# A two-layer decoder block: the order of all engines in the first attention, its PSUM banks, and its crossing into the FFN stage

## The chip, the cores and the metric

The kernel runs on one core of a Trainium2 chip. Time is device microseconds of one execution, lower is better. The engines are TensorE (PE), VectorE (DVE), ScalarE (ACT), GpSimd (POOL) and SyncE (SP, which here only issues DMAs). Each takes its own instructions in the written order, and they meet only at semaphores.

## The reference, cut to what matters

Sixteen sequences of 128 rows by 128 columns pass through four steps, each added to its input. The first one is the stage that the change touches:

```python
# x: (16, 128, 128), ctx: (16, 120, 128), H = 16 heads of 8
xn = layernorm(x)
q, k, v = xn @ Wq.T, ctx @ Wk.T, ctx @ Wv.T          # split into 16 heads
scores = einsum('bhqd,bhkd->bhqk', q, k) * SCALE      # + causal mask
attn = softmax(scores)
x = x + einsum('bhqk,bhkd->bhqd', attn, v) @ Wo.T
x = x + ternary_ffn(layernorm(x))                     # 128 -> 512 -> 128
x = x + relative_attention(layernorm(x), ctx)         # 16 heads of 64
x = x + int8_linear(layernorm(x))
```

The FFN needs its two weight matrices turned into ternary ones first (mean of the absolute values, comparison, sum with the rest). The last step needs its matrix quantised. Both are done once, in small pieces strewn among the steps of the first attention.

## The kernel before

Every engine runs three stages one after the other: `attn0` (first attention), `ffn0`, and `layer1` (second attention and last linear). Each stage is a software pipeline over the 16 sequences: at step s it works on several sequences t at once (for example scores of t = s, softmax sums and the scaling of t = s-1, the product with V of t = s-2, the output projection of t = s-3, layer norm of t = s+3 and s+4). Steps 6 to 11 of `attn0` are a hardware loop, the others are written out. The order inside a step is fixed by hand, engine by engine. `crossing` is the list of how the last steps of `attn0` and the first of `ffn0` alternate on each engine.

One step of `attn0` holds, for each sequence: on PE two pairs of masks (`causal`), two pairs of score products (32 rows of the array each, output tile 0 to 3 = head groups g of 4 heads), two groups of 16 transposes of the probabilities (64 rows), two groups of 8 products with V (`vexp`, 32 columns), three projections q, k, v, the projection `wo`, and a transpose of `xn` (all 128x128). On ACT 16 exponentials and two half copies of the transposes. On DVE four maxima (`nmax`), four reciprocals (`rsum`), two half copies (`probT` and its second half, which lies in `relr0`), copies `oT`, `qT`, `kexp` (which lies in `relw`), `v`, `xnT`, the layer-norm statistics and `xn`. On POOL four multiplications of the probabilities by `rsum` (`scaled0` to `scaled3`), `vexp`, and a power for the layer norm (`rstd`).

The pieces of work done once stand on DVE at steps 2 to 5 (comparison of `wup` and `wdn`, into `hsq` and `relw0`) and 12 to 14 (`qx`), on POOL at steps 12, 13, 14 and 17.

`after(e, sem, n)`, `freed` and `wait_ge` are waits. In `ffn0`, DVE's first instruction of step s waits for `root`, POOL's power for the layer norm of sequence s+2, and that power is in POOL's step s-1 of `ffn0`.

Of the kernel before, what the change touches and what calls it, by code (L numbers as in the profile page):

```python
# [19 lines left out]
def decoder_kernel(nc, x, ctxT, mask, wq0T, wk0T, wv0T, wo0T, wupT, wdnT, wq1, wk1, wv1, wr1, ub, vb,  # L20
# [7 lines left out]
    with ctx:  # L28
# [270 lines left out]
        def _(pool):  # L299
# [133 lines left out]
        def _(act):  # L433
# [11 lines left out]
            def attn0(s, par):  # L445
# [6 lines left out]

                t, p = s - 2, par
                if on(t):
                    act.wait_ge(A0["probT_ps"], 2 * t + 1)
# [1012 lines left out]
```

## Time and profile before

| | us |
|---|---|
| three runs | 459.0, 452.06, 458.26 |
| their median | 458.26 |
| the profiled execution | 454.79 |
| its span, first to last instruction | 453.0 |
| of it attention steps, about | 8 to 120 |
| of it the crossing into the FFN stage, about | 112 to 135 |
| mean granted TensorE clock | 0.981 |

The profile is of one execution. Its time is 1.79 us over its span, and lies between the runs' lowest and their median. Starts and durations below are of that execution.

### The profile page before, as it was taken

Reading aid. Unit: us, or ns where it says so; the run is one execution under the profiler, and the core shown is the slowest. Engines: PE = TensorE matmul, PEld = TensorE weight load, DVE = VectorE, ACT = ScalarE, POOL = GpSimd, SP = SyncE. Lnnn points to the kernel's source line nnn. Section 1 sums busy time; section 2 is a strip of 40 time slices with the busy share of each in tenths; the row PEclk is TensorE's granted clock in tenths of the full one; section 3 lists DMA queues with packets and bytes.
Section 4 is the critical chain, followed back from the end, with each engine's and each line's share of the span. In section 5 each row is a group of like instructions: output and inputs, shape, how many; then the busy total and the mean of one; then the engine's idle time right before and its main releaser. Section 6 shows DMA issues by size and latency. Waiting matters only on the chain.

```text
span 453.0 us, 16761 instructions
## 1 busy us (share of the span) xinstructions
PE 415.2 (92%) x6147; PEld 313.1 (69%) x6147; DVE 398.8 (88%) x1300; ACT 375.1 (83%) x1483; POOL 264.2 (58%) x370
## 2 busy tenths in 40 slices
PE   7999999998789998889999999989999989998871
PEld 6555556555457777778888877868887878887560
DVE  5899999989679985799789999999999999999855
ACT  1999999998845556699989989988998999898941
POOL 4388888878966640044346357447447545646775
PEclk9999999999899999999999999999999999999796
DMA  7250000000000005887447564754754754764000
GB/s 213 58 193 26 14 11 6 11 8 15 2 2 0 0 2 138 216 208 205 120 106 191 156 146 120 190 133 104 198 134 110 198 147 94 186 163 100 8 7 23
DMA packets 54392, 44.88 MB, mean 99 GB/s; under 512 B 43952, under 2 KB 49328, under 8 KB 54320
## 3 DMA queue, kind: packets, MB, share of 16 engines
q1 hardware_dynamic: 53616, 43.59, 37.8%
q8 instruction: 46, 0.75, 0.7%
q10 hardware_dynamic: 704, 0.32, 0.3%
q14 instruction: 26, 0.21, 0.2%
HBM read 22.92 MB, written 20.97 MB: 97 GB/s over the span
## 4 chain that ended last, share of the span: by engine, by line
PE 44%; DVE 44%; issue 4%; ACT 3%; POOL 2%; DMA 1%; SPq 1%; POOLq 0%; DVEq 0%; ACTq 0%
PE PS L1003 37%; DVE prob L855 3%; PE PS L1019 3%; DVE xf L906 2%; DVE prob L901 2%; PE PS L1213 2%; DVE prob L989 1%; DVE nmax L861 1%; PE PS L1179 1%; DVE prob L995 1%; DVE prob L878 1%; DVE prob L865 1%; DVE prob L867 1%; DMA wr<-in_wr 1%; DVE qu L896 1%
## 5 line engine op out<-in xcount | busy, mean ns | idle before, releaser
L381 POOL TENSOR_TENSOR prob<-prob,rsum 128x480 f32<-128x480 f32 x64 | 69.1, 1091 | 85.4 <-DVE rsum L846 80.9
L533 ACT ACTIVATE prob<-prob,nmax 128x120 f32<-128x120 f32 x256 | 102.3, 440 | 1.0 <-DVE nmax L937 1.0
L449 ACT ACTIVATE prob<-PS,nmax 128x120 f32<-128x120 f32 x256 | 89.6, 394 | 4.3 <-DVE nmax L769 2.6
L324 POOL TENSOR_TENSOR prob<-prob,rsum 128x480 f32<-128x480 f32 x64 | 62.5, 988 | 23.2 <-DVE rsum L742 12.8
L533 ACT ACTIVATION_READ_ACCUMULATOR prob<-prob,nmax 128x1 f32 x256 | 63.0, 246 | 0.0
L449 ACT ACTIVATION_READ_ACCUMULATOR prob<-PS,nmax 128x1 f32 x256 | 61.5, 240 | 0.0
L1003 PE MATMUL PS<-rT,qv 64*32 64x152 f32 x2048 | 42.7, 293 | 5.8 <-DVE uo L933 3.8
L1003 PEld LDWEIGHTS PS<-rT,qv 64*32 64x32 f32 x2048 | 30.6, 105 | 21.6 <-issue 18.5
L1003 PEld LDWEIGHTS PS<-xnT,wq 128*128 128x128 f32 x288 | 37.1, 191 | 8.8 <-issue 7.3
L1003 PE MATMUL PS<-xnT,wq 128*128 128x128 f32 x288 | 42.7, 284 | 0.1
L1003 PE MATMUL PS<-ctx,wk 128*128 128x120 f32 x288 | 41.0, 278 | 0.0
L1003 PE MATMUL PS<-wv,ctx 128*120 128x512 f32 (+1 forms) x96 | 40.3, 501 | 0.0
L1003 PE MATMUL PS<-probT,hv 120*64 120x128 f32 x512 | 36.4, 286 | 3.2 <-ACT probT L618 3.2
L1003 PE MATMUL PS<-kT,qu 64*128 64x120 f32 x512 | 35.8, 279 | 3.0 <-ACT relw L632 2.0
L1003 PEld LDWEIGHTS PS<-ctx,wk 128*128 128x128 f32 x288 | 35.9, 191 | 2.2 <-issue 2.2
L1003 PE MATMUL PS<-wo,oT_pairs 128*128 128x128 f32 x256 | 35.9, 284 | 1.0 <-ACT oT_pairs L568 1.0
L1003 PE MATMUL PS<-relw,qT 32*128 32x480 f32 x128 | 34.4, 613 | 0.4 <-DVE relw L747 0.4
L1003 PEld LDWEIGHTS PS<-probT,hv 120*64 120x64 f32 x512 | 28.3, 140 | 8.8 <-ACT probT L618 3.7
L1003 PEld LDWEIGHTS PS<-kT,qu 64*128 64x128 f32 x512 | 31.5, 188 | 4.2 <-ACT relw L632 2.6
L1003 PEld LDWEIGHTS PS<-wo,oT_pairs 128*128 128x128 f32 x256 | 31.9, 196 | 2.5 <-ACT oT_pairs L568 1.8
L1019 PEld LDWEIGHTS PS<-ident,prob 64*120 64x120 f32 x512 | 18.2, 138 | 19.1 <-issue 19.1
L416 POOL TENSOR_TENSOR rstd<-ve,mhalf 128x1 f32<-128x1 f32 x16 | 8.7, 544 | 34.4 <-DVE ve L660 34.4
(195 smaller groups left out, 1128.5 us busy)
## 6 DMA issues: line engine op xcount, KB each, us to landing
rel_scratch<-relw SPq DMA_DIRECT2D x128, 152.0 KB, 3.1
relr<-rel_scratch SPq DMA_DIRECT2D x64, 240.0 KB, 4.2
ctx<-in_ctxT SPq DMA_DIRECT2D x32, 60.0 KB, 1.9
out_x<-fin SPq DMA_DIRECT2D x16, 64.0 KB, 3.2
x_all<-in_x SPq DMA_DIRECT2D x1, 640.0 KB, 7.1
wr<-in_wr SPq DMA_DIRECT2D x1, 512.0 KB, 5.4
wq<-in_wq SPq DMA_DIRECT2D x1, 512.0 KB, 3.6
wk<-in_wk SPq DMA_DIRECT2D x1, 512.0 KB, 4.4
```

What stands on the lines that cost most here:

```text
L324: return pool.tensor_tensor(pr, pr, cols(rsum[p], g, HG).unsqueeze(2).to_broadcast([S, HG, SK]), ALU.mult)
L381: return pool.tensor_tensor(pr, pr, cols(rsum[p], g, HG).unsqueeze(2).to_broadcast([S, HG, SK]), ALU.mult)
L416: pool.tensor_tensor(rstd[p][:, 0:1], ve[p][:, 0:1], mhalf[:, :], ALU.pow).then_inc(A1["rstd"], 1)
L449: last = act.activation(cols(prob[p], n, SK), cols(scores, q, SK), ACT.Exp, bias=nmax[p][:, n:n + 1], accum_out=ssum[p][:, n:n + 1])
L533: last = act.activation(cols(pr, n, SK), cols(pr, n, SK), ACT.Exp, bias=bias[:, n:n + 1], accum_out=total[:, n:n + 1])
L855: dve.scalar_tensor_tensor(out=sc, in0=cap[p][:, :].unsqueeze(1).to_broadcast([S, HG, SK]), scalar=NEG, in1=sc, op0=ALU.add, op1=ALU.min). ...
L861: dve.tensor_reduce(out=cols(nmax[p], 1, HG), in_=heads(cols(prob[p], 1, HG * SK), HG), op=ALU.max, axis=AX.X, negate=True).then_inc(A1["n ...
L901: dve.scalar_tensor_tensor(out=sc, in0=cap[p][:, :].unsqueeze(1).to_broadcast([S, HG, SK]), scalar=NEG, in1=sc, op0=ALU.add, op1=ALU.min). ...
L906: dve.tensor_scalar(xf[p][:, :], row(x_all, t), mv3[p][:, 0:1], rstd3[p][:, :], ALU.subtract, ALU.mult)\
L1003: return pe.matmul(o, a, b, start=start, stop=stop)
L1019: last = pe.transpose(PS[0:SK, bank, q * S // 2:(q + 1) * S // 2], cols(prob[p], g * HG + q, SK)[rows], ident_sb[rows, rows])
L1213: last = pe.transpose(PS[0:SK, bank, q * S // 2:(q + 1) * S // 2], cols(prob[p], g * HG + q, SK)[rows], ident_sb[rows, rows])
```

## The change

The four compute engines get a new order within a step of `attn0`. PE's list changes the tile shape (128x128, 32 rows, 64 rows, 32 columns) 8 times in a step, where it did 9 times. PSUM banks are given out anew. POOL does `vexp` and the scaling of group 3 after the fourth reciprocal, directly before and after that of group 2. DVE does `oT` after both late maxima, and `xn` directly behind the fourth reciprocal. In `crossing`, POOL's first two `ffn0` steps move behind one more `attn0` step each, and DVE's first one moves behind `attn0(14)`. Nothing is added to or taken from the computation.

```diff
@@ -323,14 +323,8 @@
-                t, p = s - 2, par
-                if on(t):
-                    scale_probs(p, 3).then_inc(A0["scaled3"], 1)
-                t, p = s - 1, 1 - par
-                if on(t):
-                    after(pool, A0["av1"], t - 1)
-                    pool.tensor_tensor(vexp[p][:, :].rearrange("p (g c) -> p g c", g=G), v_sb[p][:, :].unsqueeze(1).to_broadcast([SK, G, D]),
-                                       vmask_sb[:, :].rearrange("p (g c) -> p g c", g=G), ALU.mult).then_inc(A0["vexp"], 1)
...
@@ -342,7 +336,10 @@
                 t, p = s - 1, 1 - par
                 if on(t):
                     pool.wait_ge(A0["rsum"], 4 * t + 4)
+                    scale_probs(p, 3).then_inc(A0["scaled3"], 1)
                     scale_probs(p, 2).then_inc(A0["scaled2"], 1)
+                    pool.tensor_tensor(vexp[p][:, :].rearrange("p (g c) -> p g c", g=G), v_sb[p][:, :].unsqueeze(1).to_broadcast([SK, G, D]),
+                                       vmask_sb[:, :].rearrange("p (g c) -> p g c", g=G), ALU.mult).then_inc(A0["vexp"], 1)
@@ -361,10 +358,10 @@
 
             def crossing():
                 attn0(14, 0)
+                attn0(15, 1)
                 ffn0(-3, 1)
-                attn0(15, 1)
+                attn0(16, 0)
                 ffn0(-2, 0)
-                attn0(16, 0)
                 attn0(17, 1)
                 ffn0(-1, 1)
                 attn0(18, 0)
...
@@ -824,8 +827,8 @@
 
             def crossing():
+                attn0(14, 0)
                 ffn0(-3, 1)
-                attn0(14, 0)
                 attn0(15, 1)
                 ffn0(-2, 0)
                 attn0(16, 0)
```

PE's own crossing is as it was; only what its FFN steps wait for follows the new banks. Three places show what the orders come to.

PE, one step of the first attention (step 3, word for word in its written order; `relr,vexp` and `probT,vexp` are the products with V, `ident,prob` the transposes). Before:

```order
L1003 MATMUL PS<-causal,ident_bf 128x480 [waits a0_probs] x2
L1003 MATMUL PS<-wo,oT 128x128 [waits attn0_output_weights,a0_oT,a0_scaled2]
L1003 MATMUL PS<-relw,qT 128x480 [waits a0_kexp]
L1019 MATMUL PS<-ident,prob 120x64 [waits a0_scaled3,a0_probT1,ident_bf_set]
L1003 MATMUL PS<-xnT,wq 128x128 [waits a0_probT0,a0_xnT,a0_ctx_loaded0]
L1003 MATMUL PS<-causal,ident_bf 128x480 [waits a0_probs] x2
L1003 MATMUL PS<-probT,vexp 32x128 [waits a0_x_done,a0_probT0]
L1003 MATMUL PS<-relw,qT 128x480 x2
L1129 MATMUL PS<-ident,xn 128x128 [waits a0_probT3,a0_xn]
L1003 MATMUL PS<-relr,vexp 32x128 [waits a0_probT3,a0_probT2]
L1019 MATMUL PS<-ident,prob 120x64 [waits a0_scaled0,a0_scaled1,a0_v,ident_bf_set]
```

After:

```order
L1006 MATMUL PS<-wo,oT 128x128 [waits attn0_output_weights,a0_oT]
L1006 MATMUL PS<-relw,qT 128x480 [waits a0_kexp,a0_scaled3]
L1022 MATMUL PS<-ident,prob 120x64 [waits a0_probT1,a0_scaled2,a0_probT0,ident_bf_set]
L1006 MATMUL PS<-probT,vexp 32x128 [waits a0_x_done,a0_vexp]
L1006 MATMUL PS<-xnT,wq 128x128 [waits a0_v,a0_xnT,a0_ctx_loaded0]
L1006 MATMUL PS<-causal,ident_bf 128x480 [waits a0_probs]
L1117 MATMUL PS<-ident,xn 128x128 [waits a0_probT3,a0_xn]
L1006 MATMUL PS<-relw,qT 128x480 x2
L1006 MATMUL PS<-relr,vexp 32x128 [waits a0_probT3,a0_probT2]
L1022 MATMUL PS<-ident,prob 120x64 [waits a0_scaled0,a0_scaled1,a0_xnT,ident_bf_set]
```

The transpose of `xn` now follows the second pair of masks, which has its own shape, and the first products with V stand ahead of the projections.

DVE at step 3 of the first attention, where one of the four pieces of FFN weight work stands (`hsq<-wup`). Before:

```order
L704 TENSOR_REDUCE nmax1<-PS 128x4 [waits a0_scores0]
L706 TENSOR_REDUCE nmax1<-PS 128x4
L721 SCALAR_TENSOR_TENSOR hsq<-wup,tiny0,hsq 128x512
L737 TENSOR_SCALAR qT0<-PS 128x128 [waits a0_qkv_ps,setup_vector]
L740 RECIPROCAL rsum0<-ssum0 128x4
L742 RECIPROCAL rsum0<-ssum0 128x4 [waits a0_probs]
```

After:

```order
L729 RECIPROCAL rsum0<-ssum0 128x4 [waits a0_probs]
L733 TENSOR_SCALAR xn0<-x_all,mv0,rstd0 128x128 [waits a0_rstd]
L748 SCALAR_TENSOR_TENSOR hsq<-wup,tiny0,hsq 128x512
L764 TENSOR_SCALAR qT0<-PS 128x128 [waits a0_qkv_ps,setup_vector]
L768 COPY xnT1<-PS 128x128 [waits a0_xnT_ps]
L773 TENSOR_TENSOR relw0<-PS,kmask 128x480
L778 TENSOR_REDUCE nmax1<-PS 128x4 [waits a0_scores1]
L780 TENSOR_REDUCE nmax1<-PS 128x4
L676 RECIPROCAL rsum1<-ssum1 128x4 [waits a0_probs]
L680 COPY oT1<-PS 128x128 [waits a0_av1]
```

The piece moved from behind two maxima to behind the fourth reciprocal (L729) and `xn`, and `oT` now comes last of the chain maxima, reciprocal, `oT`.

POOL in the crossing, around `rstd<-ve,half`, which is the `root` that DVE's FFN steps wait for. Before:

```order
L357 TENSOR_TENSOR rstd0<-ve0,half 128x2 [waits f0_var,setup_pool]
L324 TENSOR_TENSOR prob1<-prob1,rsum1 128x480
L332 TENSOR_TENSOR vexp0<-v0,vmask 120x512 [waits a0_av1]
L324 TENSOR_TENSOR prob0<-prob0,rsum0 128x480 [waits a0_rsum] x3
L357 TENSOR_TENSOR rstd1<-ve1,half 128x2 [waits f0_var]
```

After:

```order
L324 TENSOR_TENSOR prob0<-prob0,rsum0 128x480 [waits a0_rsum] x2
L324 TENSOR_TENSOR prob0<-prob0,rsum0 128x480
L341 TENSOR_TENSOR vexp0<-v0,vmask 120x512
L354 TENSOR_TENSOR rstd0<-ve0,half 128x2 [waits f0_var]
L324 TENSOR_TENSOR prob1<-prob1,rsum1 128x480 [waits a0_rsum] x3
L324 TENSOR_TENSOR prob1<-prob1,rsum1 128x480
L341 TENSOR_TENSOR vexp1<-v1,vmask 120x512
L354 TENSOR_TENSOR rstd1<-ve1,half 128x2 [waits f0_var]
L348 TENSOR_TENSOR wdn<-wdn,relw0 128x512
```

Each of the first two roots moved behind a whole attention step of POOL, the four scalings and `vexp`, and the second stands directly ahead of the last piece on `wdn`.

## Rows read from the trace of the kernel before

**Rows 1.** The chain of waits, 50 to 85 us: shares of that stretch.

```profile
by line: PE PS L1003 78.5%; PE PS L1019 18.2%; PE PS L1129 3.7%
```

**Rows 2.** Busy time of 50 to 75 us: PE, PEld, DVE, ACT, POOL, clock, DMA.

```profile
50.00:75.00 25.00, 25.00 (x307) 14.58 (x305) 23.77 (x80) 24.95 (x131) 21.24 (x23) 1.00 0.05 12
```

**Rows 3.** Timeline of PE: start, length, operation, tile, count; most of one step.

```profile
63.17 0.58 PE L1003 MATMUL PS<-causal,ident_bf 128*128 128x480 bf16 x2
63.58 0.38 PE L1003 MATMUL PS<-wo,oT 128*128 128x128 f32 x2
...
65.52 0.49 PE L1003 MATMUL PS<-xnT,wq 128*128 128x128 f32 x2
...
66.28 0.57 PE L1003 MATMUL PS<-causal,ident_bf 128*128 128x480 bf16 x2
66.78 0.64 PE L1003 MATMUL PS<-probT,vexp 120*32 120x128 f32 x16
67.36 1.07 PE L1003 MATMUL PS<-relw,qT 32*128 32x480 f32 x4
...
68.62 0.64 PE L1003 MATMUL PS<-relr,vexp 120*32 120x128 f32 x16
...
69.82 0.58 PE L1003 MATMUL PS<-causal,ident_bf 128*128 128x480 bf16 x2
```

**Rows 4.** Timeline of DVE in the same steps.

```profile
69.33 0.29 DVE L778 COPY oT<-PS 128x128 f32<-128x128 f32 x1
...
71.67 0.66 DVE L704 TENSOR_REDUCE nmax<-PS 128x4 f32<-128x480 f32 x1
72.24 0.65 DVE L706 TENSOR_REDUCE nmax<-PS 128x4 f32<-128x480 f32 x1
```

**Rows 5.** Timeline of PE at a wait for DVE; in brackets the idle time.

```profile
95.17 0.30 PE L1129 MATMUL PS<-ident,xn 128*128 128x128 f32 x1 [0.15 <-DVE relr L752]
```

**Rows 6.** Timelines of POOL and DVE: DVE operations that read SBUF, and POOL's beside them.

```profile
25.29 0.83 DVE L719 TENSOR_SCALAR hsq<-wup,tiny 128x512 f32<-128x512 f32 x1
...
32.29 0.74 DVE L721 SCALAR_TENSOR_TENSOR hsq<-wup,tiny,hsq 128x512 f32<-128x512 f32 x1
...
39.21 0.48 DVE L719 TENSOR_SCALAR relw<-wdn,tiny 128x512 f32<-128x512 f32 x1
...
20.27 0.99 POOL L324 TENSOR_TENSOR prob<-prob,rsum 128x480 f32<-128x480 f32 x1 [1.77 <-DVE rsum L742]
...
20.71 0.62 DVE L756 TENSOR_SCALAR xn<-x_all,mv,rstd 128x128 f32<-128x128 f32 x1
...
431.28 0.32 DVE L906 TENSOR_SCALAR xf<-x_all,mv_f,rstd_f 128x128 f32<-128x128 f32 x1
...
431.36 0.55 POOL L406 TENSOR_TENSOR x_all<-xb,uo 128x128 f32<-128x128 f32 x1
```

**Rows 7.** Timelines of POOL and DVE in the crossing.

```profile
113.24 0.71 POOL L357 TENSOR_TENSOR rstd<-ve,half 128x2 f32<-128x2 f32 x1
...
114.86 1.28 POOL L332 TENSOR_TENSOR vexp<-v,vmask 120x512 f32<-120x512 f32 x1
...
126.36 1.27 POOL L351 TENSOR_TENSOR wdn<-wdn,relw 128x512 f32<-128x512 f32 x1
...
116.38 0.17 DVE L765 RECIPROCAL rsum<-ssum 128x4 f32<-128x4 f32 x1
...
118.67 0.21 DVE L786 TENSOR_SCALAR tiny<-rstd 128x1 f32<-128x1 f32 x1
...
119.21 0.32 DVE L804 TENSOR_SCALAR xn<-x_all,mv,tiny 128x128 f32<-128x128 f32 x1
...
123.30 0.17 DVE L765 RECIPROCAL rsum<-ssum 128x4 f32<-128x4 f32 x1
...
125.42 1.07 DVE L804 TENSOR_SCALAR xn<-x_all,mv,tiny 128x128 f32<-128x128 f32 x1
126.41 1.24 DVE L808 TENSOR_SCALAR ve<-eps,mv 128x2 f32<-128x2 f32 x1
```

More of the change, by code:

```diff
@@ L700, in attn0 @@
                     dve.tensor_copy(ident_bf[:, :], ident_sb[:, :]).then_inc(ident_set, 1)
+                t, p = s - 2, par
+                if on(t):
+                    dve.wait_ge(A0["probT_ps"], 2 * t + 1)
+                    dve.tensor_copy(query_half(probT0[0], 1), heads(PS[0:SK, 6, :], 2 * HG)).then_inc(A0["probT1"], 1)
+                t, p = s - 1, 1 - par
+                if on(t):
+                    dve.wait_ge(A0["probs"], 4 * t + 2)
+                    dve.reciprocal(cols(rsum[p], 0, HG), cols(ssum[p], 0, HG)).then_inc(A0["rsum"], 1)
@@ L701, in attn0 @@
+                t, p = s - 3, 1 - par
+                if on(t):
+                    dve.wait_ge(A0["y_ps"], t + 1)
+                    if at_step(s, NB - 1):
+                        link(dve.tensor_copy(qrhs[:, :], PS[:, 7, D:2 * D]))
+                        link(dve.tensor_copy(rhs_scale[:, :], PS[:, 7, 2 * D:3 * D]))
+                    dve.tensor_tensor(row(x_all, t), PS[:, 7, 0:D], row(x_all, t), ALU.add).then_inc(A0["x_done"], 1)
                 t, p = s, par
                 if on(t):
+                    after(dve, A0["vexp"], t - 1)
+                    dve.tensor_copy(v_sb[p][:, :], PS[0:SK, 0, 256:256 + D]).then_inc(A0["v"], 1)
@@ new lines, in attn0 @@
+                t, p = s - 1, 1 - par
+                if on(t):
+                    dve.wait_ge(A0["probs"], 4 * t + 4)
+                    dve.reciprocal(cols(rsum[p], 3, HG), cols(ssum[p], 3, HG)).then_inc(A0["rsum"], 1)
+                t, p = s + 3, 1 - par
+                if on(t):
+                    dve.wait_ge(A0["rstd"], t + 1)
+                    dve.tensor_scalar(xn[p][:, :], row(x_all, t), mv[p][:, 0:1], rstd[p][:, 0:1],
+                                      ALU.subtract, ALU.mult).then_inc(A0["xn"], 1)
@@ L1050, in attn0 @@
                     pe.wait_ge(A0["kexp"], t + 1)
-                    for g, bank in ((0, 0), (1, 2)):
+                    for g, bank in ((0, 2), (1, 1)):
                         rows = slice(32 * g, 32 * g + 32)
@@ L1064, in attn0 @@
                 if on(t):
-                    free = held(pe, t + 1)
+                    count0 = held(pe, t + 1)
+                    count1 = held(pe, t + 1)
                     ready = held(pe, t + 1)
                     pe.wait_ge(ident_set, 1)
-                    pe.wait_ge(A0["probT1"], free)
-                    pe.wait_ge(A0["scaled3"], ready)
-                    probs_transpose(p, 2, (6, 5)).then_inc(A0["probT_ps"], 1)
+                    pe.wait_ge(A0["probT0"], count0)
+                    pe.wait_ge(A0["probT1"], count1)
+                    pe.wait_ge(A0["scaled2"], ready)
+                    probs_transpose(p, 2, (5, 6)).then_inc(A0["probT_ps"], 1)
+                if at_step(s, 2):
+                    pe.wait_ge(r_set, 4)
+                t, p = s - 2, par
+                if on(t):
+                    pe.wait_ge(A0["vexp"], t + 1)
+                    after(pe, A0["x_done"], t)
+                    for g in (0, 1):
+                        for q in range(HG):
+                            last = mm(PS[32 * q:32 * q + 32, 7, 0:S], vexp[p][:, g * D + 32 * q:g * D + 32 * q + 32],
+                                      cols(probT0[0], (g % 2) * HG + q, S), start=(g == 0), stop=(g == G - 1))
+                    last.then_inc(A0["av0"], 1)
                 if at_step(s, 1):
@@ L1096, in attn0 @@
                         pe.wait_ge(masks_loaded, 16 * 2)
-                    after(pe, A0["probs"], 4 * t)
                     mm(PS[:, 3, 0:HG * SK], ident_bf[:, :], causal_sb[:, :], stop=False)
-                if at_step(s, 2):
-                    pe.wait_ge(r_set, 4)
-                t, p = s - 2, par
+                t, p = s + 2, par
                 if on(t):
-                    pe.wait_ge(A0["probT0"], t + 1)
-                    after(pe, A0["x_done"], t)
-                    for g in (0, 1):
-                        for q in range(HG):
-                            last = mm(PS[32 * q:32 * q + 32, 7, 0:S], vexp[p][:, g * D + 32 * q:g * D + 32 * q + 32],
-                                      cols(probT0[0], (g % 2) * HG + q, S), start=(g == 0), stop=(g == G - 1))
-                    last.then_inc(A0["av0"], 1)
+                    pe.wait_ge(A0["xn"], t + 1)
+                    freed(pe, (A0["probT3"], t - 3, t - 4), (A0["xnT"], t, t - 1))
+                    pe.transpose(PS[:, 6, 0:S], xn[p][:, :], ident_sb[:, :]).then_inc(A0["xnT_ps"], 1)
                 t, p = s, par
                 if on(t):
-                    for g, bank in ((2, 3), (3, 1)):
+                    for g, bank in ((2, 3), (3, 4)):
                         rows = slice(32 * g, 32 * g + 32)
```

158 lines of the change are left out of this document (65 added, 93 removed), and 3 rows, old and new, of the table A0.

## The prediction, made before the changed kernel had run

> **What bounds it now.** I read the chain of waits over the steady attention steps first: every piece of it is PE work, none a wait for another engine [rows 1]. Then the busy times of the same stretch: PE 25.00 of 25 us, ACT 24.95, DVE 23.77, POOL 21.24, clock 1.00 [rows 2]. So PE sets the step, but nobody is far behind: DVE has 25 - 23.77 = 1.23 us idle in 3.76 steps, 0.33 us a step, and ACT shows none (its lengths stretch while it waits, so it may have some). PE's timeline gives the step: masks to masks 63.17 to 69.82, 6.65 us [rows 3]. A gain on PE can be no more than what the nearest other engine leaves.
>
> **PE's changes of shape.** The price of one is read from two pairs of the same masks. The pair at 63.17, followed by another 128x128 product, takes 0.41 us until the next start; that at 66.28, followed by products of another shape, takes 66.78 - 66.28 = 0.50 [rows 3]. So a change costs 0.09 us. One of nine goes (masks to the transpose of `xn`): PE's own work becomes 6.65 - 0.09 = 6.56 us a step. Over the 16 steps this is at most 1.5 us, 0.3%. The bounds of a change are 0.05 and 0.15, by the other joints in PE's timeline, hence 0.8 to 2.4 us. I take 1.5 as the gain on offer.
>
> **Who takes it back: the wait for `oT`.** In the new order a loop closes over PE and DVE: the late scores end, DVE takes two maxima, a reciprocal and `oT`, and only then may PE do `wo` and all that follows to the next late scores. Its length, by start to start: `wo`, early scores and 16 transposes 63.58 to 65.52, 1.94 us; first V products 66.78 to 67.36, 0.58; projections 65.52 to 66.28, 0.76; masks without a change 0.41; transpose of `xn` and late scores to their end, 67.36 to 68.62 and the 0.07 by which the scores' 1.07 exceeds 1.00, 1.33 [rows 3]. PE's part is 5.02. DVE's: two maxima of 72.24 - 71.67 = 0.57 each, a reciprocal that holds the next start for half of its 0.17, say 0.09, `oT` 0.29, and about 0.04 to start behind the scores: 1.56 [rows 4, 7]. Then PE restarts behind a wait for DVE with 0.15 idle [rows 5]. Sum 6.73 us, against 6.65 before and 6.56 on PE alone. The 0.15 is of a place where the shape changes too, which `wo` behind the masks does not; without the 0.09 of that it is 0.06, and the sum 6.64. So the step will be 6.6 to 6.75. I take 6.67: the loop is worth +0.02 a step, +0.3 us in 16 steps, bounds -1.2 and +2.4. The gain on PE is thus given back in a wait for `oT`, a resource that the old order had early.
>
> **The work done once, steps 2 to 5.** Here the queue matters. DVE's fourth reciprocal releases three POOL operations at a stroke in the new order (scaling 3, scaling 2, `vexp`), and behind it on DVE stand `xn` and then the weight piece. Rows show that such a DVE operation does not run beside a POOL one: `xn` started at 20.71, 0.44 us into a scaling that ran to 21.26, and took 0.62 where the like of it took 0.32 at 119.21; in the crossing one took 1.07 [rows 6, 7]. The blocked `xn` ended 0.07 us behind POOL's end (21.33 against 21.26); a 512-wide piece has more to do once it is let in, by estimate its own length less some 0.2 of start: 0.3 for a comparison (0.48), 0.55 for a three-operand piece (0.74). In the old place the four pieces took 0.83, 0.74, 0.48 and 0.74 us, the last alike the second [rows 6]. In the new place `xn` starts when half of the reciprocal's 0.17 us is over and POOL's first scaling when all of it is, 0.08 behind `xn`; it is itself held a little, say 0.1, and with its 0.99 ends about 1.17 behind `xn`'s start; so the two comparisons end at 1.47 from `xn`'s start and the two three-operand pieces at 1.72. Without that block they would end at 0.25 + their old length, 1.08, 0.73, 0.99 and 0.99. The difference is 0.39 + 0.74 + 0.73 + 0.73 = 2.6 us. DVE's slack of 0.33 a step was used up by the pieces themselves before, so the 2.6 pass on in full; if half a step's slack is still there it is 1.5. I take 2.6, bounds 0.5 and 3.5.
>
> The Trainium skill (SBUF — State Buffer, section "SBUF: two separate sides") says that VectorE and GpSimd share one port pair as an exclusive lock for a whole instruction, which goes to whoever starts first, when VectorE works in a two-port mode or with two SBUF inputs. The trace agrees at 20.71. By that rule the step's `xn` itself is at risk too, in all 13 steps; without the rule this edit would cost nothing, and the sum would be 2.6 us lower.
>
> **The crossing.** Before, POOL did the first root at 113.24, long before DVE asked at 118.67 [rows 7]. Now POOL's first root stands behind two scalings and `vexp` that wait for the fourth reciprocal of sequence 14. With that reciprocal where it was, 116.38: it ends at 116.55, then 0.95, 0.95 and 1.23 us (the 0.99 and 1.28 of the rows, less the overlap of one with the next) and the root of 0.71 give 120.4; DVE goes on at 120.45 instead of 118.67, +1.8 us. DVE stands still there with the last softmax work queued behind: the reciprocals, `oT` and the half copies of sequence 15 and 14, for which POOL and PE wait. Second round, first `xn` to second: DVE reaches the fourth reciprocal of sequence 15 after 3.0 us if nothing disturbs it (`ve`, reciprocal, `oT` and the first half copy 1.3, PE's 16 transposes and the restart 0.9, the second half copy and the reciprocal 0.8; before it took 123.30 - 119.21 = 4.09 with waits in it [rows 7]), then 0.17, again 3.84 on POOL, 0.54 from root to `xn` (119.21 - 118.67): 7.5 us, against 125.42 - 119.21 = 6.21. That is +1.3, up to +2.4. Third round: before, `xn` and `ve` at 125.42 and 126.41 took 1.07 and 1.24, held by a scaling and by the piece on `wdn` [rows 7]. Now the `wdn` piece starts at the root's end and holds `xn` alone, to about 1.35 behind the root; before it was 127.65 - 124.88 = 2.8 to the end of `ve`. It saves 1.2. Together +1.9. PE idles longer there and its granted clock may fall; I add nothing for that, but let the upper bound go to +5; the lower is 0. Steps 12 to 14 with the `qx` pieces are DVE-bound before and after, and I put them at 0, as I do the prologue (steps -4 to 1), where each new wait meets work that is one or two sequences short: +0.5, bounds -0.5 and +1.
>
> **The sum.** 0.3 + 2.6 + 1.9 + 0.5 = +5.3 us. FFN and second attention are unchanged and move along. Against the profiled execution: 454.79 + 5.3 = 460.1. That execution lies 3.5 us under the median of the runs shown (458.26) and the four times have a mean of 456.0; with the change on these two it is 461.3 to 463.6. I forecast **462 us**, 0.9% over the median, which is less than a measurement of this kernel tells from no change (2%, 9.2 us).
>
> **Rival 1, the lock falls the other way in the loop: slower beyond 2%.** `xn` starts 0.08 us ahead of POOL's scaling in every step, because both follow the same reciprocal. If POOL gets the SBUF port first, `xn` takes 1.07 instead of 0.34, as at 125.42 [rows 7]: 0.73 more on DVE, 0.33 of it slack, and with the `oT` loop behind it nearly all the rest in the step: 0.4 to 0.7 us in 13 steps, 5 to 9 us on top of the 5.3, so 467 to 472. Against it speaks a pair of the same spacing: at 431.28 DVE's `xf` started 0.08 before POOL's `x_all` and kept its 0.32 us, and it was POOL that was stretched, to 0.55 [rows 6]. It decides once the reciprocal's signal comes early or `xn` late by about 0.1 us. Chance 0.15.
>
> **Rival 2, the change brings what it looks like: not slower.** Then the wait for `oT` is short enough (DVE's 1.56 hidden), POOL's scalings leave gaps that the weight pieces fit into, and in the crossing the reciprocals come earlier than before by as much as the roots come later. The time is -1.5 from the shapes and -1 to +1 from the rest: 455 to 458. For it speaks that PE now asks for scaling 3 with one of the step's later waits. Against it speak DVE's 23.77 of 25 us even without the pieces [rows 2]. Chance 0.25.
>
> **Rival 3, the gain is larger than the shapes.** If ACT and DVE had been held by PE and both have real slack, a step could fall to the 6.3 us of DVE's own work: 16 times 0.3, 5 us, to 453. The busy times of 24.95 for ACT speak against it. Chance 0.05.
>
> **Chances.** The forecast has 0.55. The range takes in the forecast's own bounds, the lower part of rival 1 and rival 2: 454 to 470. Faster by over 2% needs under 449.1: 0.03. Slower by over 2%, over 467.4: rival 1 and the upper end of the crossing, 0.19. The rest, 0.78, is within.
>
> **What would show it.** In the profile after: PE in the loop with one idle stretch of about 0.1 us before `wo`, ended by DVE `oT`, and a step of 6.6 to 6.8; `xn` at 0.34 in the loop (1.07 for rival 1); the four weight pieces at 1.0 to 1.5 us instead of 0.48 to 0.83; DVE idle 2 to 4 us twice in the crossing, ended by POOL's `rstd<-ve,half`; and all of the FFN stage about 5 us later than before. I am wrong if PE shows no wait for `oT`, if the pieces keep their lengths, or if DVE's waits for the root are short.

## The result and the profile after

| | before | after |
|---|---|---|
| median of the runs, us | 456.64 | 461.26 |
| their range, us | 452.06 to 459.0 | 458.3 to 463.32 |
| profiled execution, us (span) | 454.79 (453.0) | 462.51 (460.7) |
| mean granted clock | 0.981 | 0.966 |

The ratio is 1.0105, 95% interval 1.0056 to 1.0153: some 4.8 us slower, less than 2%. (Ratios here and below leave disturbed executions out, so they can differ a little from a quotient of medians.) The two profiled executions lie 7.7 us apart, more than the ratio says: that of before is among the quickest of its kernel, with a mean granted clock of 0.981, that of after among the slowest, with 0.966. Over many executions the clocks do not differ so. The four of after have 0.966, 0.978, 0.964 and 0.976 (in the order 462.51, 458.3, 463.32, 460.02 us), 0.971 in the mean; the 72 executions of the kernel before that count in the ratios of the experiments have 0.970 in the mean. So the profiled pair overstates what the clock does to this change, and its stretches are to be read with that in mind.

To find where the 7.7 us are, take from PE's timelines the end of `wo` for each sequence (`y0` to `y15` below) and the start of the fifth FFN sequence's `up` product.

| stretch | before, us | after, us | difference | predicted |
|---|---|---|---|---|
| start to y0 (prologue) | 30.10 | 30.82 | +0.72 | +0.5 |
| y0 to y4 (the four weight pieces) | 27.22 | 29.40 | +2.18 | +2.6 |
| y4 to y10 (loop) | 40.07 | 40.27 | +0.20 | +0.3 in 16 steps |
| y10 to the fifth `up` (crossing) | 40.36 | 45.13 | +4.77 | +1.9 |
| the rest | 315.21 | 315.08 | -0.13 | 0 |

**The loop.** One step of PE and DVE after the change, from the timeline of the kernel after (start, length, engine, line, operation; PE weight loads are PEld), and behind it a row of its waits from 55 to 90 us:

```profile
72.64 0.58 PE L1006 MATMUL PS<-causal,ident_bf 128*128 128x480 bf16 x2
72.70 0.17 DVE L676 RECIPROCAL rsum<-ssum 128x4 f32<-128x4 f32 x1
72.79 0.26 DVE L680 COPY oT<-PS 128x128 f32<-128x128 f32 x1
...
73.10 0.30 PEld L1006 LDWEIGHTS PS<-wo,oT 128*128 128x128 f32 x2 [0.35 <-DVE oT L680]
```

```profile
PEld PS L1006 <- DVE oT L680: 1.8, 5, 0.4
```

The row of waits reads: 1.8 us in total, 5 times, at most 0.4 us; it is the weight load (PEld) that waits.

A step earlier DVE's `xn` and POOL's scaling, which follow the same reciprocal:

```profile
63.19 0.32 DVE L733 TENSOR_SCALAR xn<-x_all,mv,rstd 128x128 f32 x1
...
63.35 1.00 POOL L324 TENSOR_TENSOR prob<-prob,rsum 128x480 f32<-128x480 f32 x1 [0.76 <-DVE rsum L729]
```

`xn` starts 0.16 us ahead and keeps its length, as forecast (with 0.08 us). `wo` is ready to go when the masks have been issued (in the old order it followed them at 0.41 us, [rows 3]); now it starts 0.46 us behind them (73.10 - 72.64), when `oT` is through, and reciprocal and `oT` run directly ahead of it, behind DVE's maxima. The two `wo` products then hold the next start for 0.42 us (73.10 to 73.52), where they held it for 0.32 (63.58 to 63.90), as PE's timelines show, after and before:

```profile
73.52 1.07 PE L1006 MATMUL PS<-relw,qT 32*128 32x480 f32 x4
```

```profile
63.90 1.07 PE L1003 MATMUL PS<-relw,qT 32*128 32x480 f32 x4
```

PE is no longer full, as the busy times show (PE, PEld, DVE, ACT, POOL, then the clock); PE was 25.00 and ACT 24.95 before [rows 2]:

```profile
50.00:75.00 25.00, 24.16 (x313) 13.79 (x311) 23.71 (x80) 23.57 (x123) 20.96 (x22) 1.00 0.05 11
```

**Steps 2 to 5.** Timelines of DVE and POOL at two of the four pieces; the other two read alike (1.21 and 1.48):

```profile
26.36 0.32 DVE L733 TENSOR_SCALAR xn<-x_all,mv,rstd 128x128 f32<-128x128 f32 x1
26.59 1.21 DVE L746 TENSOR_SCALAR hsq<-wup,tiny 128x512 f32<-128x512 f32 x1
...
26.52 2.12 POOL L324 TENSOR_TENSOR prob<-prob,rsum 128x480 f32<-128x480 f32 x2 [0.75 <-DVE rsum L729]
...
33.98 1.48 DVE L748 SCALAR_TENSOR_TENSOR hsq<-wup,tiny,hsq 128x512 f32<-128x512 f32 x1
...
33.91 2.39 POOL L324 TENSOR_TENSOR prob<-prob,rsum 128x480 f32<-128x480 f32 x2 [0.77 <-DVE rsum L729]
```

DVE's piece begins 0.07 us behind POOL's first scaling and takes 1.21 (comparison) and 1.48 (three operands), where the comparisons took 0.83 and 0.48 in the old place and the three-operand pieces 0.74 [rows 6]. POOL's pair of scalings stretches from 1.93 (the pair at 121.23, below) to 2.12 and 2.39.

**The crossing.** Timeline of DVE, POOL and PE there:

```profile
120.98 0.17 DVE L729 RECIPROCAL rsum<-ssum 128x4 f32<-128x4 f32 x1
...
125.09 0.21 DVE L789 TENSOR_SCALAR tiny<-rstd 128x1 f32<-128x1 f32 x1 [0.79 <-POOL rstd L354]
...
125.64 0.31 DVE L807 TENSOR_SCALAR xn<-x_all,mv,tiny 128x128 f32<-128x128 f32 x1
...
133.05 0.21 DVE L789 TENSOR_SCALAR tiny<-rstd 128x1 f32<-128x1 f32 x1 [3.93 <-POOL rstd L354]
...
133.60 0.72 DVE L807 TENSOR_SCALAR xn<-x_all,mv,tiny 128x128 f32<-128x128 f32 x1
...
121.23 1.93 POOL L324 TENSOR_TENSOR prob<-prob,rsum 128x480 f32<-128x480 f32 x2 [3.89 <-DVE rsum L729]
123.12 1.27 POOL L341 TENSOR_TENSOR vexp<-v,vmask 120x512 f32<-120x512 f32 x1
124.35 0.71 POOL L354 TENSOR_TENSOR rstd<-ve,half 128x2 f32<-128x2 f32 x1
...
115.50 0.47 PE L1044 MATMUL PS<-ident,qx 128*128 128x128 f32 x1 [1.66 <-DVE oT L680]
...
116.76 1.97 PE L1006 MATMUL PS<-relw,qT 32*128 32x480 f32 x4
```

Two things are to be seen. POOL's root comes directly behind two scalings and `vexp` that the fourth reciprocal released, its end 4.1 us behind the reciprocal's start, and DVE stands still for it. And the late scores at 116.76 take 1.97 us, where they take 1.07 at full clock [rows 3]. This follows PE's wait of 1.66 us for `oT`, but not of necessity: with POOL's old list (experiments 4 to 7) the same scores, behind the same wait of 1.65 us, took 1.07. The windows of the same stretch have the granted clock (third number from the end):

```profile
115.00:120.00 5.00, 4.50 (x33) 2.74 (x37) 3.13 (x12) 1.87 (x10) 2.10 (x3) 0.55 0.00 0
120.00:125.00 5.00, 4.22 (x54) 1.86 (x46) 2.37 (x5) 4.48 (x24) 3.77 (x4) 0.77 0.00 0
125.00:130.00 5.00, 3.89 (x51) 2.87 (x51) 3.09 (x15) 3.75 (x13) 2.79 (x4) 0.58 0.02 5
130.00:135.00 5.00, 3.54 (x29) 1.84 (x21) 1.95 (x9) 1.22 (x4) 4.64 (x6) 0.74 0.00 0
```

### The profile page after: what moved, and what is told of

The parts are those of the page before. It is cut to its first block, busy times and chain, and to the rows that moved or that the text cites. A ratio compares the mean times of both kernels' runs of the same rounds, so it can differ in the third digit from the quotient of the medians.

```text
span 460.7 us, 16767 instructions
## 1 busy us (share of the span) xinstructions
PE 422.5 (92%) x6147; PEld 315.8 (69%) x6147; DVE 399.5 (87%) x1300; ACT 374.6 (81%) x1483; POOL 265.9 (58%) x370
## 4 chain that ended last, share of the span: by engine, by line
DVE 40%; PE 23%; ACT 3%; issue 3%; POOL 1%; POOLq 0%; DVEq 0%; ACTq 0%
PE PS L1006 20%; DVE prob L858 3%; DVE xf L909 3%; DVE prob L904 2%; DVE prob L992 2%; DVE nmax L864 2%; DVE prob L998 2%; DVE prob L881 1%; DVE prob L868 1%; DVE prob L870 1%; DVE nmax L940 1%; DVE nmax L948 1%; DVE qu L955 1%; DVE qu L899 1%; DVE kT L945 1%
## 5 line engine op out<-in xcount | busy, mean ns | idle before, releaser
L533 ACT ACTIVATION_READ_ACCUMULATOR prob<-prob,nmax 128x1 f32 x256 | 64.3, 251 | 0.0
L447 ACT ACTIVATION_READ_ACCUMULATOR prob<-PS,nmax 128x1 f32 x256 | 63.7, 249 | 0.0
L1006 PE MATMUL PS<-relw,qT 32*128 32x480 f32 x128 | 35.6, 633 | 1.1 <-DVE relw L773 1.1
L1006 PEld LDWEIGHTS PS<-kT,qu 64*128 64x128 f32 x512 | 31.5, 188 | 4.2 <-ACT relw L632 2.6
```

The lines of the kernel that those rows point to most:

```text
L447: last = act.activation(cols(prob[p], n, SK), cols(scores, q, SK), ACT.Exp, bias=nmax[p][:, n:n + 1], accum_out=ssum[p][:, n:n + 1])
L533: last = act.activation(cols(pr, n, SK), cols(pr, n, SK), ACT.Exp, bias=bias[:, n:n + 1], accum_out=total[:, n:n + 1])
L1006: return pe.matmul(o, a, b, start=start, stop=stop)
```

## Experiments

All but two are the changed kernel with one edit or a few. Besides the ratio, which counts for the sum, each has the stretches of its one profiled execution. For reference, y0 to y4, one loop step (y4 to y9 by 5) and the crossing are 27.22, 6.65 and 40.36 before, 29.40, 6.68 and 45.13 after.

**1. The weight pieces early.** The whole block of the four pieces moves, in DVE's step, from behind `xn` to ahead of the second early maximum, that of group 0:

```diff
+                for k, w, change in ((0, wup_sb, hsq[:, :]), (1, wdn_sb, relw[0][:, 512:512 + DFF])):
+                    if at_step(s, 2 + 2 * k):
+                        link(dve.tensor_scalar(change, w[:, :], tiny[k][:, 2:3], None, ALU.is_lt))
...
                 t, p = s, par
                 if on(t):
                     dve.tensor_reduce(out=cols(nmax[p], 0, HG), in_=heads(PS[:, 2, 0:HG * SK], HG),
...
-                for k, w, change in ((0, wup_sb, hsq[:, :]), (1, wdn_sb, relw[0][:, 512:512 + DFF])):
-                    if at_step(s, 2 + 2 * k):
-                        link(dve.tensor_scalar(change, w[:, :], tiny[k][:, 2:3], None, ALU.is_lt))
...
```

> The changed kernel with one thing moved: DVE's four pieces of FFN weight work (steps 2 to 5) stand ahead of the fourth maximum and the fourth reciprocal instead of behind xn, so that no POOL scaling is under way beside them. If they were held by POOL in the new place (they took 1.21, 1.48, 1.21 and 1.48 us there), they take 0.45 to 0.75 each here, and the kernel is 2 to 3 us faster than the changed one, with steps 2 to 5 of the first attention about 0.7 us shorter each. If the holding by POOL is hidden work (the rival), their lengths may fall but the times of the output projections from step 7 on stay within 0.5 us.

Ratio 1.0062 (1.0022 to 1.0103), median 459.49. y0 to y4 27.23, step 6.68, crossing 44.18. Timeline of DVE, one piece of each kind:

```profile
25.82 0.48 DVE L724 TENSOR_SCALAR hsq<-wup,tiny 128x512 f32<-128x512 f32 x1
32.50 0.74 DVE L726 SCALAR_TENSOR_TENSOR hsq<-wup,tiny,hsq 128x512 f32<-128x512 f32 x1
```

The pieces have their lengths back and the whole 2.2 us of the four steps is gone: the cost was the place of the pieces. The ratios differ by 0.43%, 2.0 us, which fits, but the two intervals overlap, so that the stretch shows it and the timed runs alone would not.

**2. Who starts first (`xn` behind `qT`).**

```diff
-                t, p = s + 3, 1 - par
-                if on(t):
-                    dve.wait_ge(A0["rstd"], t + 1)
-                    dve.tensor_scalar(xn[p][:, :], row(x_all, t), mv[p][:, 0:1], rstd[p][:, 0:1],
-                                      ALU.subtract, ALU.mult).then_inc(A0["xn"], 1)
...
                     dve.tensor_scalar(qT[p][:, :], PS[:, 0, 0:S], SCALE0, None, ALU.mult).then_inc(A0["qT"], 1)
+                t, p = s + 3, 1 - par
+                if on(t):
+                    dve.wait_ge(A0["rstd"], t + 1)
+                    dve.tensor_scalar(xn[p][:, :], row(x_all, t), mv[p][:, 0:1], rstd[p][:, 0:1],
+                                      ALU.subtract, ALU.mult).then_inc(A0["xn"], 1)
```

> The changed kernel with DVE's xn taken after qT instead of right behind the fourth reciprocal, so that POOL's scaling has begun when xn starts. Theory (who starts first holds the SBUF port): POOL's scalings keep 1.0 us or less, xn takes 0.9 to 1.1 us instead of 0.32, and the loop's step grows from 6.68 to 6.8 to 7.1 us, 3 to 5 us in all; the weight pieces no longer stand behind the same release and shorten. Rival (no exclusive port, the stretch is only sharing of bandwidth): xn stays under 0.5 us wherever it starts.

One profile, 462.17 us. Timelines of POOL and DVE in the loop, then DVE's two kinds of pieces, which now follow the reciprocal directly, as `xn` did:

```profile
62.68 1.93 POOL L324 TENSOR_TENSOR prob<-prob,rsum 128x480 f32<-128x480 f32 x2 [0.75 <-DVE rsum L729]
...
62.68 0.29 DVE L759 TENSOR_SCALAR qT<-PS 128x128 f32<-128x128 f32 x1
62.89 0.86 DVE L763 TENSOR_SCALAR xn<-x_all,mv,rstd 128x128 f32 x1
...
26.80 0.46 DVE L741 TENSOR_SCALAR hsq<-wup,tiny 128x512 f32<-128x512 f32 x1
...
33.88 0.72 DVE L743 SCALAR_TENSOR_TENSOR hsq<-wup,tiny,hsq 128x512 f32<-128x512 f32 x1
```

`xn` started 0.21 us behind POOL and took 0.86 instead of 0.32; it ended at 63.75, just behind POOL's first scaling (62.68 + 0.99 = 63.67). POOL's pair kept its 1.93. The pieces, now ahead of POOL, kept 0.46 and 0.72. The step grew to 6.89, +0.21. So DVE pays when it starts second, and rival 1 is a real mechanism, from which `xn`'s lead of 0.16 us keeps the change. Sharing of bandwidth is out: by the expectation `xn` would have stayed under 0.5, and POOL would have been stretched as well. What POOL pays when it starts second is hardly seen in the loop: 0.16 us behind `xn` its scaling took 1.00 for 0.99.

**3. `oT` between the two late maxima.**

```diff
-                t, p = s - 3, 1 - par
-                if on(t):
-                    dve.wait_ge(A0["av1"], t + 1)
-                    dve.tensor_copy(oT[p][:, :], PS[:, 7, 0:S]).then_inc(A0["oT"], 1)
...
+                t, p = s - 2, par
+                if on(t):
+                    dve.wait_ge(A0["av1"], t + 1)
+                    dve.tensor_copy(oT[p][:, :], PS[:, 7, 0:S]).then_inc(A0["oT"], 1)
+                t, p = s, par
+                if on(t):
                     dve.tensor_reduce(out=cols(nmax[p], 3, HG), in_=heads(PS[:, 4, 0:HG * SK], HG),
```

> The changed kernel with DVE's copy oT between the two late maxima instead of behind both and the next reciprocal, about 0.5 us earlier. If the wait for oT alone gives the gain of the shapes back, the loop's step falls from 6.68 to 6.56 to 6.60 us and PE's idle time before the output projection goes; the kernel is 1 to 1.5 us faster. If another wait is just behind it (the rival: the transposes wait for DVE's half copy probT, which stands behind the same maxima), the idle time moves there and the step stays at 6.64 to 6.70.

Ratio 1.0095 (1.0052 to 1.0139), median 459.65. Timeline of PE:

```profile
67.71 0.58 PE L1008 MATMUL PS<-causal,ident_bf 128*128 128x480 bf16 x2
68.12 0.39 PE L1008 MATMUL PS<-wo,oT 128*128 128x128 f32 x2
...
69.67 0.69 PE L1024 MATMUL PS<-ident,prob 64*120 64x64 f32 x16 [0.16 <-issue]
```

`wo` follows the masks at 0.41 us, with no wait: so it was `oT` that held it. But 16 transposes now wait 0.16 us, for which the profile names no releaser, and the step is 6.72, neither the 6.56 to 6.60 of the theory nor quite the 6.64 to 6.70 of the rival. Here a wait that goes has another directly behind it; which one, experiment 9 tells.

**4 to 7. The lists of the crossing, apart and together.** The edits in the changed kernel, POOL's first and then DVE's; the other two runs put them, the other way round, into the kernel before:

```diff
             def crossing():
                 attn0(14, 0)
+                ffn0(-3, 1)
                 attn0(15, 1)
-                ffn0(-3, 1)
+                ffn0(-2, 0)
                 attn0(16, 0)
-                ffn0(-2, 0)
...
             def crossing():
+                ffn0(-3, 1)
                 attn0(14, 0)
-                ffn0(-3, 1)
                 attn0(15, 1)
```

> The changed kernel with the crossing lists of POOL and DVE as before (POOL's first two powers for the FFN's layer norm one attention step earlier), the order within a step new. If DVE's waits for that power are what the crossing costs, the attention steps up to 14 are as in the changed kernel, DVE's first wait of 0.8 us and second of 3.9 us go, PE's clock drops for less than the 17 us of the changed kernel, and the time is 4 to 6 us lower. If the loss in the crossing comes from the order within the steps (the rival: PE waits 1.7 us for oT at step 15 and its clock falls there, before either power is asked for), it is 0 to 2 us lower.

> The changed kernel with POOL's order in the crossing alone as in the kernel before: each FFN root before the scalings of the attention step. Theory (the late roots are the loss): DVE's two waits for rstd, 0.79 and 3.93 us, go, the crossing falls from 45.1 to 38 to 41 us, ratio 0.998 to 1.003. Rival (the loss needs only DVE's list, or both): the waits for the root stay or other waits of the same length take their place, ratio 1.006 or more.

> The changed kernel with DVE's order in the crossing alone as in the kernel before: the first FFN sequence's xn and statistics are taken one attention step earlier; POOL's roots stay behind its scalings. Theory (POOL's roots come too late, whoever asks): DVE asks for the root even earlier and stands still longer; the crossing from sequence 10 to the fifth up product stays at 44 to 47 us, ratio 1.009 to 1.016. Rival (DVE's list is the culprit, POOL's is harmless as it was in the kernel before): crossing 38 to 41 us, ratio 0.998 to 1.003.

> The kernel before with POOL's crossing list alone taken from the changed kernel (each FFN root one attention step later). Theory (the roots behind the scalings make DVE's xn wait, and PE's wait costs clock): nothing moves up to sequence 12; DVE idles 2 to 4 us before two of the FFN's xn, PE's idle stretches there grow and more of the crossing runs at half clock; FFN starts 2 to 5 us later, ratio 1.004 to 1.011. Rival (the roots come in time in the old loop order, the loss needs the new order of the loop): under 1 us, ratio 0.998 to 1.002.

> The kernel before with both crossing lists, POOL's and DVE's, taken from the changed kernel. With POOL's alone the crossing was 41.0 us against 40.4. Theory (the pair of new lists is bad with either loop order): crossing 43 to 46 us, ratio 1.004 to 1.010. Rival (the lists were chosen for the order of the loop and are bad or good only with it): crossing 40 to 42 us, ratio 0.996 to 1.003.

| loop order | POOL's list | DVE's list | crossing, us | its mean clock | ratio (interval) |
|---|---|---|---|---|---|
| new | new | new | 45.13 | 0.81 | 1.0105 (1.0056 to 1.0153) |
| new | new | old | 43.50 | 0.92 | 1.0141 (1.0084 to 1.0198) |
| new | old | new | 37.93 | 0.96 | 0.9995 (0.9955 to 1.0034) |
| new | old | old | 37.77 | 0.95 | 0.9999 (0.9947 to 1.0050) |
| old | old | old | 40.36 | 0.96 | 1 |
| old | new | old | 40.99 | 0.96 | 0.9966 (0.9926 to 1.0005) |
| old | new | new | 40.90 | 0.92 | 0.9981 (0.9935 to 1.0028) |

It is POOL's list that costs: with it as before the crossing is 7.2 us shorter and the kernel 1.1% faster, or 5.7 us and 1.4% with DVE's old list; both ratios differ by more than their intervals. DVE's list makes no difference that the intervals tell. And it costs only in the new loop order: in the old one it is worth 0.6 us in the profile and nothing in the timed runs, so that there the theory fell and the rival held. The timelines say why. Changed kernel with POOL's old list, POOL and DVE:

```profile
115.12 0.71 POOL L354 TENSOR_TENSOR rstd<-ve,half 128x2 f32<-128x2 f32 x1 [0.17 <-DVE ve L811]
...
122.65 0.70 POOL L354 TENSOR_TENSOR rstd<-ve,half 128x2 f32<-128x2 f32 x1 [0.30 <-DVE ve L811]
...
120.96 0.20 DVE L789 TENSOR_SCALAR tiny<-rstd 128x1 f32<-128x1 f32 x1
...
125.10 0.18 DVE L789 TENSOR_SCALAR tiny<-rstd 128x1 f32<-128x1 f32 x1
```

Kernel before with both new lists, POOL and DVE:

```profile
115.34 3.06 POOL L324 TENSOR_TENSOR prob<-prob,rsum 128x480 f32<-128x480 f32 x3
118.36 0.71 POOL L357 TENSOR_TENSOR rstd<-ve,half 128x2 f32<-128x2 f32 x1
...
116.95 0.17 DVE L765 RECIPROCAL rsum<-ssum 128x4 f32<-128x4 f32 x1
...
119.10 0.21 DVE L786 TENSOR_SCALAR tiny<-rstd 128x1 f32<-128x1 f32 x1 [0.29 <-POOL rstd L357]
```

In the old loop order the fourth reciprocal releases only scaling 2, the last of the three at 115.34; scaling 3 and `vexp` stand in POOL's next step, behind the root, which starts 1.4 us after the reciprocal. In the new order all three stand between the reciprocal and the root, the root starts 3.4 us after it (124.35 against 120.98), and POOL had been idle for 3.89 us before. The new list is harmless until the loop order loads the fourth reciprocal.

**8. The clock.** Products of PE with no use, 8 masks at step 15 and 8 and 7 products of 128x128 ahead of the first two waits for the FFN's `xn`:

```diff
+                    if at_step(s, 15):
+                        for _ in range(8):
+                            mm(PS[:, 1, 0:HG * SK], ident_bf[:, :], causal_sb[:, :])
...
+                    for _ in range(8 if at_step(t, 0) else 7 if at_step(t, 1) else 0):
+                        mm(PS[:, p, S:2 * S], mean_w[:, :], mean_w[:, :])
                     pe.wait_ge(F0["xn"], t + 1)
```

> The changed kernel with extra PE products whose results are not used (8 of the masks at step 15 ahead of the wait for oT, 8 and 7 of 128x128 ahead of the waits for the first two FFN layer norms), so that PE is not idle in the crossing. If the half clock that the changed kernel shows from 115.5 to 122.3, 125.7 to 132.6 and 136.0 to 139.4 us follows from those idle times and costs time, the clock stays at 1.00 for most of the crossing and the kernel is 2 to 4 us faster, although PE has 5 us more work. If the half clock lies beside waits for POOL anyway (the rival), the clock rises but the time changes by under 1 us.

Ratio 1.0103 (1.0044 to 1.0161), median 460.82. The crossing in the profile: 42.13 us, clock 0.96 (0.81 without). Two of its windows, and DVE's two waits:

```profile
115.00:120.00 5.00, 4.96 (x53) 2.70 (x53) 4.67 (x16) 3.33 (x17) 4.16 (x4) 1.00 0.08 14
...
125.00:130.00 5.00, 3.60 (x50) 2.62 (x52) 2.99 (x15) 3.17 (x11) 2.83 (x4) 0.75 0.01 2
```

```profile
125.32 0.21 DVE L789 TENSOR_SCALAR tiny<-rstd 128x1 f32<-128x1 f32 x1 [2.00 <-POOL rstd L354]
...
133.23 0.21 DVE L789 TENSOR_SCALAR tiny<-rstd 128x1 f32<-128x1 f32 x1 [3.92 <-POOL rstd L354]
```

At the clock of before (0.96) the crossing of the changed kernel is 42.13 against 40.36, +1.8 us (with whatever the unused products themselves cost); the other 3.0 of the 4.8 in the profiled pair come with the lower clock. The waits for the root are all there, 2.00 and 3.92. But the timed runs do not show the 3 us: 1.0103 against 1.0105, each uncertain by 0.5 to 0.6%.

The mean clocks say why. A mean clock gives, as an estimate, the time at half clock: twice its distance from 1, times the span. For the four executions of the changed kernel that is 31, 20, 33 and 22 us, in the order of their times above. In each of the 14 profiles of this case 13 us of it or more lie behind 420 us, far from the changed stage (16 in that of the changed kernel, which had 17 in the crossing and none elsewhere). So the executions of 458.3 and 460.02 us had at most some 7 and 9 us at half clock ahead of that: the bad crossing came in two executions of four at most. And the kernel before has more of it than its profile shows: its mean of 0.970 is 27 us, against 17 in its profiled execution. So the difference in the timed runs, 4.8 us, is in the main not one of the clock. The stretches without the clock add up to it: 0.7 for the prologue, 2.2, 0.2 and 1.8 make 4.9.

**9. Putting together what helped.** The pieces early and both crossing lists as before; then `oT` between the maxima as well; then also DVE's statistics of `x` (L652 to L660) behind its half copy of `probT`:

```diff
+                t, p = s - 2, par
+                if on(t):
+                    dve.wait_ge(A0["probT_ps"], 2 * t + 1)
+                    dve.tensor_copy(query_half(probT0[0], 1), heads(PS[0:SK, 6, :], 2 * HG)).then_inc(A0["probT1"], 1)
                 t, p = s + 4, par
                 if on(t):
...
                     norm_stats(A0, t, p)
...
-                t, p = s - 2, par
-                if on(t):
-                    dve.wait_ge(A0["probT_ps"], 2 * t + 1)
-                    dve.tensor_copy(query_half(probT0[0], 1), heads(PS[0:SK, 6, :], 2 * HG)).then_inc(A0["probT1"], 1)
```

> The changed kernel with two edits at once: DVE's four FFN-weight pieces taken ahead of the first early maximum, and POOL's and DVE's order in the crossing as in the kernel before. Theory (the loss sits in these two places and they are independent): about 2.4 us of the loop's entry and 5 us of the crossing come back together; the FFN stage then begins 1 to 2 us earlier than in the kernel before, ratio to it 0.994 to 0.999. Rival (each alone only uncovers what the other hides, or the loop's order costs by itself): no better than the better of the two alone, ratio 1.000 to 1.005.

> As the kernel with both edits, and DVE's oT copy put between the two late maxima too. Theory: the idle time before wo goes, but a wait before the transposes takes its place (+0.03 us a step, as seen with that edit alone), while sequences 9 to 12 save 2 us or so; net 1 to 2 us less than without it, ratio 0.990 to 0.997. Rival: the +0.03 us in each step and a held DVE elsewhere eat it; same as without it, within 0.3%.

> The best kernel so far (pieces early, both crossing lists as before, oT between the late maxima: ratio 0.9916) with one more edit: DVE's statistics of x taken behind its copy of half of probT, for which PE waited 0.16 us a step. Theory: that wait shortens, step 6.60 to 6.68 instead of 6.71, 1 to 1.5 us less, ratio 0.986 to 0.990. Rival (the statistics are wanted early, so the wait moves to xn; or the 0.16 us had another cause): step and ratio unchanged or up to 1 us worse, 0.990 to 0.994.

| | step, us | crossing, us | median, us | ratio (interval) |
|---|---|---|---|---|
| pieces and lists | 6.68 | 40.34 | 453.97 | 0.9953 (0.9921 to 0.9985) |
| and `oT` | 6.71 | 37.58 | 453.39 | 0.9916 (0.9890 to 0.9943) |
| and the statistics | 6.55 | 39.70 | 452.67 | 0.9898 (0.9864 to 0.9931) |

The first gives the sum of its parts: from 1.0105 down by 1.52%, where the pieces alone gave 0.43 and the lists alone 1.06. The last is 1.0% faster than the kernel before, the first 0.5%. From row to row the intervals overlap, and the crossings ran at mean clocks of 0.87, 0.95 and 0.87, so that only the steps tell one edit from the next. The last one's busy times from 50 to 75 us and PE's timeline in the loop:

```profile
50.00:75.00 25.00, 24.90 (x322) 14.83 (x322) 23.99 (x81) 25.00 (x131) 21.37 (x24) 1.00 0.06 12
```

```profile
66.26 0.57 PE L1008 MATMUL PS<-causal,ident_bf 128*128 128x480 bf16 x2
66.67 0.27 PE L1119 MATMUL PS<-ident,xn 128*128 128x128 f32 x1
66.87 1.07 PE L1008 MATMUL PS<-relw,qT 32*128 32x480 f32 x4
...
69.07 0.58 PE L1008 MATMUL PS<-causal,ident_bf 128*128 128x480 bf16 x2
69.48 0.39 PE L1008 MATMUL PS<-wo,oT 128*128 128x128 f32 x2
```

PE has hardly any idle time (24.90 of 25 us busy), and the step is 6.55: 0.10 less than before, the price of one shape change. The masks are followed at 0.41 us in both places, without a change of shape in the first. The 0.16 us wait of experiment 3 was thus for DVE's half copy of `probT`, which stood behind the statistics once `oT` no longer kept PE back.

## Why the prediction was right, and where it was off

It said 462 us, 454 to 470, within 2% with 0.78. Measured: 461.26, ratio 1.0105. The sum was +5.3 us, measured +4.8. That the forecast itself is met to 0.7 us is in part luck: four executions of one kernel spread over 5 us. (462 is 0.8% over the median of 458.26, not 0.9.)

- **The gain on offer, 0.09 us a step: right.** With the waits removed the step is 6.55 against the 6.56 predicted for PE alone.
- **The wait for `oT` gives it back: right.** Step 6.68 for 6.67, one wait before `wo` ended by `oT`. The prediction looked at this one wait only, and another was directly behind it: taking `oT` forward alone gave 6.72, as the half copy of `probT` was next.
- **The pieces: right in mechanism, 0.4 us too dear.** +2.2 for +2.6. They took 1.21 and 1.48 against estimates worked from `xn`'s start, 1.47 and 1.72, which from the same start are 26.59 + 1.21 - 26.36 = 1.44 and 1.71. So nearly all of the difference is not in the pieces: some 0.3 us did not pass on to PE. That points to slack in DVE's step, which I had put at nothing; no run tried it. The Trainium skill (SBUF — State Buffer, section "SBUF: two separate sides") has the pair of ports as a lock that whoever starts first keeps for its whole instruction. The traces agree for DVE in both directions: 0.16 us ahead it kept its 0.32, 0.21 us behind it took 0.86. That POOL is blocked when it comes second shows in its pair of scalings (2.12 and 2.39 for 1.93 beside a piece), but not behind `xn`, where it took 1.00 for 0.99.
- **Rival 1, the lock the other way: did not happen.** Its price was 0.4 to 0.7 us a step; experiment 2 measured 0.21. DVE's `xn` took 0.54 more, not 0.73, as it was let in behind a scaling that had begun 0.21 us earlier, and 0.33 of slack was there.
- **The crossing: right at equal clock, far off in the profiled pair.** "Together +1.9. PE idles longer there and its granted clock may fall; I add nothing for that". In the profiled pair it was +4.8. Round by round: from the fourth reciprocal to DVE's restart 4.11 us for 4.07 predicted (125.09 - 120.98); but that reciprocal came at 120.98, where 116.38 [rows 7] and the 3.1 us of delay so far make 119.5: 1.5 us late. PE's work ahead of it ran at half clock: from PE's restart behind `oT` at 115.50 to the reciprocal it was 5.48 us, and 3.66 in the two runs in which the same work ran at full clock (with POOL's old list 115.29 to 118.95, with the unused products 117.56 to 121.22). So the first round cost 3.3 instead of 1.8. The second, `xn` to `xn`, was 133.60 - 125.64 = 7.96 for 7.5, +1.75 against the 6.21 of before instead of +1.3. The third gave back 0.3 and not 1.2 (from that `xn` to the fifth `up` 12.02 for 12.33). With the unused products, at before's clock, the three rounds are +1.5, +1.7 and -1.4 for the predicted +1.8, +1.3 and -1.2, and the crossing +1.8. The two idle times of DVE, forecast at 2 to 4 us, are 2.00 and 3.92 there, and 0.79 and 3.93 in the profiled execution. So what I priced was right in its sum and nearly in its parts; the 3.0 us that I left to the upper bound are in the profiled pair, and the timed runs do not show them.
- **The +1.9 is also a net of two larger things that I did not see.** With POOL's old list the new order crosses in 37.9 us, 2.4 less than before, and the late roots cost 4.2 on top of that at the same clock. The 2.4 are saved from y13 on: y13 to y15 takes 9.88 us there (9.93 and 9.72 with both old lists, without and with the early pieces) and 12.48 before, the other steps together as much as before. Experiment 9 does not keep it: with `oT` and then the statistics moved it is 10.78 and 13.04. In that stretch PE's timeline of before has two waits ahead of transposes, 1.28 us for POOL's scaling and 1.13 with no releaser named; with POOL's old list in the new order its waits are of 0.3 us. That these are the 2.4 was not tried by a run.
- **Prologue:** +0.72 in this pair for +0.5. In the profiles in which the first 15 us ran at full clock, y0 was 29.6 to 31.6 us in the new order and 30.10 and 30.33 in the old, so the term is about as large as its scatter.

## What to carry to other kernels

When operations are regrouped behind one signal, as here scaling 3, scaling 2 and `vexp` behind the fourth reciprocal, look at what else stands behind that signal on the same queue (a root for another engine) and at what starts on the neighbour engine at the same moment (a 512-wide piece): the two largest costs lay there, and neither in the loop for which the order was chosen. A gain on the bounding engine is only there after each wait behind it has been moved in turn: here `oT`, then the half copy of `probT`, and with both the promised 0.10 us a step came. And where a change lets the matmul engine idle in a short stretch, a single profile can charge it with 3 us of clock that the mean of many executions does not have: compare such stretches at one mean clock, and compare the mean clocks of all timed executions before the clock gets a term in the sum.

## What the runs showed of the hardware

- The same instructions cross in 37.77 or 40.34 us, by where the half clock falls. The kernel with both old lists and the one that has the pieces early as well have one code from step 6 on, but in the profile of the second more of the crossing ran at half clock (mean 0.87 against 0.95). Behind one and the same wait of 1.54 us for `oT` the score products took 1.07 us in the first (full clock) and 1.97 in the second (half clock). So 2.6 us of a crossing can be the clock alone, and of the crossings in the tables above only differences well over that, or at one mean clock, say something.
- In some executions PE runs at half clock for part of the prologue, and in others not, whatever the kernel. Windows from 10 to 15 us, the changed kernel and then the one with the unused products, whose prologue is the same code:

```profile
10.00:15.00 5.00, 4.88 (x27) 3.20 (x24) 4.30 (x10) 3.31 (x17) 0.54 (x1) 1.00 0.68 203
```

```profile
10.00:15.00 5.00, 4.05 (x14) 3.53 (x15) 2.85 (x5) 2.48 (x11) 0.09 (x1) 0.66 0.66 202
```

  y0 then is 32.88 instead of 30.82 us; over all profiles it is 31.5 to 32.9 us in the five with such a prologue and 29.6 to 31.6 in the nine without. These 2 us are a good part of the scatter between executions of one kernel, and a single profile of each kernel can differ by them before the changed code has run at all: differences are to be taken from stretch to stretch.
